# Local attention stage of a 12-stage transformer kernel: softmax steps queued over half a round, weight evictions behind them

## The reference, cut to what matters

```
_OFFSETS = list(range(41)) + [128, 48, 192]
B, T, C, H = (1, 256, 128, 16)          # x of the whole chain: 2048 tokens x 128 channels
q, k, v = split(layernorm(x) @ w_qkv)   # 16 heads of 8
score[t, j, h] = q[t, h] . (k[t - off_j, h] * scaled embedding_j) + pos_bias[j, h]
p = softmax over the 44 offsets j (offsets that reach before the start are masked)
y[t, h] = gain_h * sum_j p[t, j, h] * v[t - off_j, h]
x = x + y @ w_out
```

## Time and profile before

| what | value |
|---|---|
| median of 3 runs | 3794.89 us (3793.42 to 3797.33) |
| the profiled execution, its own time | 3791.39 us |
| its span, first to last instruction | 3789.6 us |
| mean granted PE clock | 0.923 of 2.4 GHz |
| busy over the span: PE, DVE, ACT, POOL | 88%, 71%, 49%, 28% |
| the changed stage's rounds 1 to 4 | about 163 to 540 us of the span |

### The profile page before, as it was taken

How to read it: one execution, slowest core, us unless ns; L and a number is a source line. 1 busy time by engine, 2 the same in 40 slices (tenths; PEclk the granted TensorE clock), 3 DMA queues, 4 the chain that set the end, 5 groups by cost and what they waited for, 6 DMA issues and landing times. The chain is left out here.

```text
span 3789.6 us, 55832 instructions
## 1 busy us (share of the span) xinstructions
PE 3340.8 (88%) x21901; PEld 1713.5 (45%) x21909; DVE 2680.4 (71%) x5708; ACT 1868.3 (49%) x3374; POOL 1051.6 (28%) x832
## 2 busy tenths in 40 slices
PE   4678875899979999999889988888999899899899
PEld 3222234566642333333356655656676322333577
DVE  8787778777759999999387773454435787884433
ACT  2232222677745777777667772223222366666321
POOL 0244560867631000000096660001202111311100
PEclk9779987999988999999999998989999798999899
DMA  0000000311100000000031110000200000000100
GB/s 21 9 0 1 0 1 1 87 27 34 26 5 1 1 1 1 1 1 1 11 81 30 30 23 24 6 24 23 71 1 28 1 1 1 1 1 1 46 1 12
DMA packets 49631, 60.16 MB, mean 16 GB/s; under 512 B 9364, under 2 KB 34328, under 8 KB 49240
## 3 DMA queue, kind: packets, MB, share of 16 engines
q1 hardware_dynamic: 49368, 56.59, 5.4%
HBM read 39.22 MB, written 1.10 MB: 11 GB/s over the span
## 5 line engine op out<-in xcount | busy, mean ns | idle before, releaser
L142 PE MATMUL ps<-AR 128*128 128x128 f32 (+8 forms) x16848 | 2137.1, 434 | 156.3 <-DVE AR L114 36.9
L131 ACT ACTIVATE AR<-ps 128x512 f32<-128x512 f32 (+6 forms) x1808 | 1280.8, 749 | 1169.5 <-PE ps L142 887.7
L142 PEld LDWEIGHTS ps<-AR 128*128 128x128 f32 (+5 forms) x16848 | 1031.2, 152 | 1293.3 <-DVE AR L125 410.2
L125 DVE TENSOR_REDUCE AR<-ps 128x1 f32<-128x512 f32 (+1 forms) x1424 | 936.4, 709 | 96.3 <-PE ps L142 95.7
L114 POOL TENSOR_TENSOR AR<-AR 128x512 f32<-128x512 f32 (+4 forms) x422 | 552.4, 1323 | 655.9 <-ACT AR L131 418.2
L131 ACT ACTIVATE AR<-ps,AR 128x128 f32<-128x128 f32 (+2 forms) x700 | 355.9, 527 | 318.8 <-PE ps L142 292.4
L114 POOL TENSOR_TENSOR rs<-rs,halves 128x4 f32<-128x4 f32 x64 | 68.0, 1063 | 1494.7 <-DVE rs L118 1494.0
L142 PE MATMUL ps<-XT,AR 128*128 128x512 f32 x896 | 439.8, 627 | 18.9 <-DMA AR<-in_L3f_w 7.6
L114 DVE TENSOR_TENSOR AR<-ps,AR 128x512 f32<-128x512 f32 (+3 forms) x626 | 299.1, 528 | 127.0 <-PE ps L142 89.7
L122 DVE SCALAR_TENSOR_TENSOR X<-ps,AR,X 128x128 f32<-128x128 f32 x512 | 143.7, 344 | 342.4 <-PE ps L142 342.1
L150 PE MATMUL ps<-C,AR 128*128 128x128 f32 (+1 forms) x1593 | 254.1, 297 | 105.4 <-DVE AR L114 44.3
(11 more groups left out here) (83 smaller groups left out, 1890.1 us busy)
## 6 DMA issues: line engine op xcount, KB each, us to landing
AR<-AR SPq DMA_DIRECT2D x124, 128.0 KB, 2.3
AR<-in_c_rot SPq DMA_DIRECT2D x64, 128.0 KB, 2.2
AR<-in_L3f_w SPq DMA_DIRECT2D x32, 256.0 KB, 5.8
AR<-in_L2f_w SPq DMA_DIRECT2D x32, 128.0 KB, 2.7
AR<-scr_bias SPq DMA_DIRECT2D x32, 128.0 KB, 3.2
WR<-in_c_rot SPq DMA_DIRECT2D x4, 512.0 KB, 5.5
WR<-in_L_ffn_wqkv SPq DMA_DIRECT2D x2, 768.0 KB, 4.8
AR<-in_L_ffn_wqkv SPq DMA_DIRECT2D x2, 768.0 KB
```

The lines of the kernel that those rows point to most:

```text
L125: return self.do(lambda e: e.tensor_reduce(o, a, AXX, op, negate=neg, apply_absolute_value=mag), *w)
L131: return self.do(lambda e: e.activation(o, a, f, bias=bias, scale=scale, accum_out=acc), *w)
L142: last = e.matmul(o, l, r, start=a, stop=z, skip_group_check=True)
```

## The change

Only the positions of two lists in a round change. The softmax steps, until now between 0 and 0.25 of the round, go between 0 and 0.5; the drops, until now between 0.4 and 1, go between 0.55 and 1. No instruction is added, removed or altered, and no wait: only the order in each engine's queue in rounds 1 to 4.

```diff
     for n in range(6):
         soft, drops = soft_steps(n - 1) if 1 <= n <= 4 else ([], [])
-        weave((value_steps(n - 2) if n >= 2 else [], 0, 1), (soft, 0, 0.25), (drops, 0.4, 1),
+        weave((value_steps(n - 2) if n >= 2 else [], 0, 1), (soft, 0, 0.5), (drops, 0.55, 1),
               (score_steps(n) if n < 4 else [], 0.1, 1))
```

## The result

The changed kernel takes 3811.19 us (median of 5 runs, 3807.98 to 3817.95) against 3796.88 us for the kernel before in the same comparison; the ratio is 1.0047 with a 95% interval of 1.0036 to 1.0059. The change makes it slower by some 0.5%, outside the range I gave. The profiled execution took 3808.36 us.

The account below looks back on a forecast made before the run. Heads (before drop 0) were taken as DVE's time, tails as PE's. Rounds 1 to 4 at +3.3, -1.4, -1.4 and +0.2 sum to +0.7 us, giving 3796 us; range 3784 to 3808 us.

Parts of the forecast that it names:

- the likeliest case: Whole kernel: time within 0.2% (7.6 us) of the kernel before, chance 0.54, with a sum of +0.7 us.
- The second rival: Split 3 before drop 0, on PE: POOL's late splits hold drop 0, +20 us, 3816 us; chance 0.19.
- the sign that I had named for being wrong: Rounds 2 and 3: the prediction is wrong if they change by over 4 us each.
- Round 2 and 3, the tail: From drop 0 on, PE's starts fall from 54.3 to 43.6 us, so the tail loses 10.7 us.
- Round 2 and 3, the head: Up to drop 0, 5 DVE products and 6 spread products add 9.3 us, bounds 7.5 to 11.9 us.
- beside them: Heads of rounds 2 and 3: two moved POOL products and three POOL additions lie beside DVE's work, adding nothing.
- A head is DVE's time: Before drop 0 DVE is the limit: busy 51.2 of 52.4 us in round 2's head, PE only 36.6.
- Round 1: Round without values: head +7.5, given back 3.3, tail -0.9, net +3.3 us; bounds -0.8 to +6.6 us.
- given back: Round 1, norm 3's end to drop 0: the lag of 8.5 us shrinks to 5.2, returning 3.3 us.
- Round 4: Round without scores: head +2.5, drops, bound by bank 4's round trip, -2.3; net +0.2 us, bounds -1.8 to +3.
- The first rival: Products behind norm 3, rounds 1 to 3: wider splits free DVE, 4.1 us a round, 3783 us; chance 0.22.
- The third rival: Heads of rounds 2 and 3: at a clock of 0.55 PE binds, each head grows 7 us, 3810 us; chance 0.05.

Follow-up runs that it names:

- e1: Kernel before with only the drops moved, to 0.55 to 1, softmax left at 0 to 0.25: 3803.7 us, ratio to before 1.0030.
- e14: e1 with POOL's additions of value pairs on 64 of their 512 columns (most of the values' sum left out): 3792.5 us.
- e9: Changed kernel with POOL's additions of value pairs on 64 of their 512 columns (most of the values' sum left out): 3791.8 us.
- e5: Changed kernel with the drops alternating between PSUM banks 4 and 3: 3809.4 us, ratio to before 1.0038.
- e3: Kernel before with each split queued right behind its norm: 3785.7 us, ratio to before 0.9985.
- e2: Changed kernel with each split queued right behind its norm: 3808.7 us, ratio to before 1.0048.
- e7: Kernel before with the softmax stretched to 0 to 0.35 and the drops left at 0.4 to 1: 3810.4 us, ratio to before 1.0041.
- e13: e7 with each split queued right behind its norm: 3789.9 us, ratio to before 1.0003.
- e12: Kernel before with each split queued right behind its norm and drops alternating between banks 4 and 3: 3781.8 us, ratio to before 0.9972.

## Why the prediction was wrong

- **The forecast** was +0.7 us in a range of 3784 to 3808 us; measured 3811.2, or +14.3. The sign of the likeliest case was right by chance, its size was not. By rounds the forecast was +3.3, -1.4, -1.4 and +0.2 us and the measurement +6.2, +3.3, +3.3 and +4.9, so over half of the miss lies in rounds 2 and 3. The second rival (3816 us, 0.19) came nearest in its number, and drop 0 did wait for POOL in rounds 1 and 4, 6.1 and 8.5 us. But in rounds 2 and 3, where I had named a wait of over 4 us as its sign, it is 0.7 and 0.8 us, and e1, without any such wait, is already 11 us slower than before: its number came near by luck. Nor did the sign that I had named for being wrong show (over 4 us in each of rounds 2 and 3; it is 3.3); it was set too wide.
- **Round 2 and 3, the tail:** -10.7 us forecast, measured -12.4. Right, by counting PE's starts.
- **Round 2 and 3, the head:** the term that was mis-sized. I priced the moved steps at 9.3 us of DVE's time and put their two POOL products and three additions at nothing, "beside them". They cost 14.2 us (e1) and 15.7 us with the softmax stretched, over my upper bound of 11.9 us. "A head is DVE's time" held only up to the end of the splits. Behind that PE needs 11.6 us by its own starts for the same steps, so the head could not have grown by 9.3: pricing them on DVE alone is the step that failed. The additions that I had put at nothing account for 1.5 us (14.2 to 12.7, e14); what the last 1.1 us are is open. Round by round the forecast was -1.4 us, the drops' half alone gave +1.9 and +1.6, the whole +3.3.
- **Round 1:** +3.3 forecast, +6.2 measured. The five products were priced well (7.5 us; the head grew by 6.9 in e1). The 3.3 us "given back" failed, and the step is this: "5.2 us must follow norm 3 if split 2 is done by then, which the wider spacing of the norms allows". It can't be done by then at any spacing, since ACT's queue has norm 3's copy ahead of split 2's. The lag from norm 3's end to drop 0 is 7.8 us instead of 5.2. ACT's order makes 1.65 us of that difference; the rest is that split 2 began on POOL only 2.5 us ahead of norm 3's end. I had followed the chain on DVE and POOL and not the queue of the third engine it passes. In e1, where the splits end early, the gathers hold drop 0 as long, so there was nothing to give back either way. The tail, forecast 0.9 us shorter, became 0.2 us longer: in e1 it is 1.9 us shorter, and the changed kernel loses 2 us of that to the clock (last section).
- **Round 4:** +0.2 forecast, +4.9 measured; the head grew by 6.7 instead of 2.5 us, the drops shrank by 1.8 instead of 2.3. The steps behind norm 3 here take 12.0 us where I had about 6: POOL runs from 508.5 to 531.7 with no gap over 0.96 us, with additions of value pairs queued between the splits. With these additions short (e9) the steps still take 10.0 us, so they explain 2 of the 6 us. That the drops are held by bank 4 was right (e5: 5.0 us less with two).
- **The first rival** (products freed of POOL) is refuted: the mean score product (its larger group) rose from 1.15 to 1.17 us in round 2's head, and without the stretch (e1) it is 1.04. The working by the port's lock, that spreading the same POOL work frees nothing, told this rightly.
- **The third rival** (cold PE) did not come in the heads, where the granted clock is 0.72 and 0.80 instead of 0.61 and 0.77. A lower clock cost time in the tails of rounds 1 and 4, which no rival had; see the last section.
- **The working of the sum** priced the steps on one engine where another needed longer (rounds 2 and 3), and laid the chain behind norm 3 too short (rounds 1 and 4). The bounds of the sum, built from DVE's products alone, could not hold either miss.

Round 5, which the change leaves alone, takes 33.9 us instead of 32.4 in the changed kernel. The kept traces tell what goes with this: in the executions of before, e1, e3 and e5 it has a granted clock of 1.00 and takes 32.4 us, in those of the changed kernel, e2, e7 and e13 it has 0.95 and takes 33.6 to 34.1 us. What stays open is why the clock falls there in some, and why the stages behind it give some 3 us back in the changed kernel's profiled execution.

## What to carry to other kernels

Price a step that is moved on every engine that it occupies, in the place where it lands; the largest of these sums is the least that it can cost. Work that lies "beside" another engine's is free only where its own engine has room. A chain of steps over three engines is as late as the latest queue that it passes: look for an instruction of the next tile queued ahead of this tile's on the engine in the middle. Here moving split k ahead of norm k+1 brought 7 us (e3) and turned a stretch of the softmax from +16 us into no loss (e13), and a second PSUM bank for a copy-out chain brought 4 us more in round 4 (e12). The same move in the changed kernel brought nothing (e2), where it also pushed POOL's products back: whoever moves steps forward on a full engine has to ask who waits for the ones behind them.

## What the runs showed of the hardware

A wait of PE can cost more than its length. In the changed kernel PE waits 6.07 us ahead of round 1's drops; the granted clock of the tail is then 0.93. The first two drops' transposes take 0.63 and 0.66 us instead of 0.42, the first two runs of gathers 1.91 and 1.77 us instead of 1.05, and all drops together take 29.99 us. In e1 the same drops with the same gathers, without such a wait, have a granted clock of 1.00 and take 27.94 us (first line; the second is round 4's tail, 25.2 us of drops against 27.2 in the changed kernel at 0.89):

```profile
211.42:241.44 30.02, 29.66 (x138) 9.17 (x137) 12.77 (x20) 15.08 (x26) 3.68 (x3) 1.00 0.00 1
...
522.87:550.33 27.46, 22.07 (x134) 11.05 (x133) 10.68 (x16) 13.51 (x23) 11.19 (x9) 1.00 0.00 1
```

So about 2 us come on top in each of these rounds: that is the whole difference between e1's and the changed kernel's tail in both (30.0 and 32.1 us; to the addition to X, 27.5 and 29.5 us). The wait need not be at the drops themselves: in e2's round 1 PE stands still for 8.6 us and then runs one stretch of gathers ahead of drop 0. The granted clock of its tail is 0.95 and the tail takes 31.5 us.
